# A 13x13 depthwise convolution on TensorE: from 18 matmuls a channel to 15, the two half-empty shifts joined into one

## What is computed

```python
def _L1_conv_ref(x, w_large, w_small, g_l, b_l, m_l, v_l, g_s, b_s, m_s, v_s, g_i, b_i, m_i, v_i):
    ...   # _dwconv: one filter per channel; _bn: scale and shift per channel
    kl = w_large.shape[-1]      # 13
    ks = w_small.shape[-1]      # 3
    out = _bn(_dwconv(x, w_large, kl // 2), g_l, b_l, m_l, v_l) + _bn(_dwconv(x, w_small, ks // 2), g_s, b_s, m_s, v_s) + _bn(x, g_i, b_i, m_i, v_i)
    return out

x = x + _L0_conv_ref(_gn(x), ...)
x = x + _L1_conv_ref(_gn(x), ...)
```

## Time and profile before

| | |
|---|---|
| median of 3 runs | 3048.57 us |
| the profiled execution's own time | 3045.88 us |
| its span, first to last instruction | 3044.2 us |
| busy share of the span: PE, DVE, ACT, POOL | 90%, 80%, 45%, 1% |
| mean granted TensorE clock | 0.981 of full speed |
| depthwise stage: PE's first matmul to the end | 2061.6 to 3044.2 us |
| mean DMA rate, 2170 to 2500 us | 280 GB/s |

### The profile page before, as it was taken

The page is one execution under the profiler, slowest core; times in us unless marked ns, Lnnn a source line. Parts: engine busy times, 40 slices in busy tenths (PEclk is TensorE's granted clock), DMA queues, the critical chain, the costliest instruction groups (busy, mean ns, idle before and its releaser), DMA issues. The chain is left out here.

```text
span 3044.2 us, 51281 instructions
## 1 busy us (share of the span) xinstructions
PE 2745.2 (90%) x18425; PEld 2007.7 (66%) x18425; DVE 2435.4 (80%) x3319; ACT 1382.1 (45%) x1729; POOL 29.0 (1%) x46
## 2 busy tenths in 40 slices
PE   0059999999999999999968999948999999999998
PEld 0036666666666666666645666637999999999997
DVE  7958999999999999999987898947565566666563
ACT  0044445555555555544224777745444444444442
POOL 0010000000000000000000000000000000000000
PEclk9999999999999999999989999969999999999999
DMA  9964111111111111110027999959988988999986
GB/s 336 416 212 150 49 64 62 65 66 62 66 67 60 66 68 59 66 61 16 16 75 236 340 344 345 348 169 281 288 281 281 282 272 279 278 286 279 286 248 186
DMA packets 228823, 564.24 MB, mean 185 GB/s; under 512 B 29248, under 2 KB 134464, under 8 KB 225600
## 3 DMA queue, kind: packets, MB, share of 16 engines
q1 hardware_dynamic: 211392, 495.41, 50.7%
q10 hardware_dynamic: 17280, 66.85, 5.8%
HBM read 402.21 MB, written 159.99 MB: 185 GB/s over the span
## 5 line engine op out<-in xcount | busy, mean ns | idle before, releaser
L1510 PE MATMUL cv_cb<-cv_hi,cv_toep 128*128 128x288 f16 (+1 forms) x4608 | 909.9, 290 | 31.6 <-DVE cv_lo L1444 28.8
L743 PE MATMUL qk_qb<-qk_xhi,whi 128*128 128x384 f16 x2592 | 846.9, 327 | 20.7 <-DVE qk_xlo L639 14.3
L743 PE MATMUL qk_qb<-qk_xlo,whi 128*128 128x384 f16 x2592 | 846.8, 327 | 0.0
L743 PE MATMUL qk_qb<-qk_xhi,wlo 128*128 128x384 f16 x2592 | 846.7, 327 | 0.0
L660 DVE SCALAR_TENSOR_TENSOR qk_dw<-qk_pool,qk_wd,qk_dw 128x768 f32<-128x768 f32 (+2 forms) x864 | 836.6, 1009 | 2.5 <-ACT qk_dw L528 2.4
L1510 PE MATMUL cv_cb<-cv_lo,cv_toep 128*128 128x288 f16 (+1 forms) x2304 | 667.6, 290 | 0.0
L1510 PEld LDWEIGHTS cv_cb<-cv_hi,cv_toep 128*128 128x128 f16 x4608 | 522.6, 113 | 91.7 <-DVE cv_lo L1444 28.9
L647 DVE TENSOR_REDUCE qk_pool<-qk_qb 128x192 f32<-128x768 f32 x432 | 412.0, 954 | 69.4 <-PE qk_qb L743 53.2
L1398 ACT ACTIVATE cv_res<-cv_cb,cv_cst 128x288 f32<-128x288 f32 x384 | 191.9, 501 | 555.3 <-PE cv_cb L1510 555.3
L1456 DVE COPY cv_rows<-cv_bb 128x512 f32<-128x512 f32 x216 | 145.7, 686 | 323.3 <-PE cv_bb L1491 323.3
L743 PEld LDWEIGHTS qk_qb<-qk_xhi,whi 128*128 128x128 f16 x2592 | 254.1, 98 | 184.3 <-DVE qk_xlo L639 17.8
(11 more groups left out here) (150 smaller groups left out, 2284.2 us busy)
## 6 DMA issues: line engine op xcount, KB each, us to landing
cv_toep<-toeplitz_scratch SPq DMA_DIRECT2D x384, 384.0 KB, 4.8
patch_scratch<-pr_turned SPq DMA_DIRECT2D x75, 832.0 KB, 9.5
cv_raw<-patch_scratch SPq DMA_DIRECT2D x24, 2600.0 KB, 10.7
st_x<-in_x SPq DMA_DIRECT2D x24, 2304.0 KB, 17.1
qk_xf<-in_x SPq DMA_DIRECT2D x72, 768.0 KB, 4.2
pr_xb<-in_x SPq DMA_DIRECT2D x24, 2304.0 KB, 10.0
out<-cv_rows ACTq DMA_DIRECT2D x72, 768.0 KB, 5.5
pr_vb<-v_scratch SPq DMA_DIRECT2D x24, 576.0 KB, 4.3
```

Source lines behind the costliest of these rows:

```text
L743: ins = nc.tensor.matmul(qbank[s % NQB][:, h, 0:2 * W], w[:, b, o * P:(o + 1) * P], x[:, par, j // 2, b, at_row:at_row + 2 * W], start=n = ...
L1510: ins = nc.tensor.matmul(out, toep[:, c % NTOEP, :].rearrange("p (s m v) -> p s v m", s=NS, m=P)[:, s, u * 2 + part], x[:, par, c, u:u + O ...
```

## The change

The depthwise stage runs 15 matmuls a channel. The padding of the Toeplitz layout is moved, and the partitions of a patch are ordered in two halves: the first 64 hold its first 4 rows, the last 64 the other 4. Shifts s = 0 and s = 1 stay as they are, 12 matmuls. What the third patch down still has to give are its first 4 rows, and they reach only the first 4 rows of the output. So for u = 0 and u = 1 these 64 partitions are put on top of each other, in `hi_last` and `lo_last`, and three matmuls with 128 input rows and 64 output columns (`late` taps) take the place of six.

- ACT copies `hi[0:64]` twice a quad into `hi_last`, DVE copies `lo[0:64]` twice a quad into `lo_last`; one of the two copies changes partitions.
- DVE writes the normalised channel into a new tile `norm` in the order channel, j, i; the border is zeroed by two instructions instead of four. `hi` and `lo` are made from `norm` and have one buffer each. The quad of a group is split when PE is done with the same quad of the group before (`free`), and quad 3 of group g in step g itself ("L3" second in ORDER).
- `toep` has 2048 bytes a partition instead of 3072; it is loaded in two halves of 64 partitions (1536 and 2048 bytes), `raw` too. `late` is one more load per quad, 128 partitions by 4 runs of 256 bytes.
- In the qkv stage POOL lays out the late taps, 6 copies for each of 16 offsets ix (the first 6 at the start), and SP sends them to DRAM, 6 transfers an offset in 256-byte runs, two offsets in each of units 2 to 9.
- POOL clears the part of `toep` that no load writes.

```diff
@@ stage_qkv, SyncE: at the end of a unit's step
+                if inner:
+                    for ix in (t * 2 - 4, t * 2 - 3):
+                        for b in range(CB):
+                            address(sp, ix * (HALF_ROWS * ERUN), 2)
+                            sp.wait_ge(late_made, ix * (2 * CB) + 2 * b + 2)
+                            for u in range(NU):
+                                windows = bass.AP(late, (b * NU + u) * EROWS * TW * 2,
+                                                  [[CB * NU * EROWS * TW * 2, P], [TW * 2, HALF_ROWS], [1, ERUN]])
+                                sp.dma_start(edge_dram[b * P:(b + 1) * P, u, bass.ds(ix, 1), :, :]
+                                             .rearrange("p a y n -> p (a y) n"), windows).then_inc(late_out[b], 16)
@@ stage_qkv, GpSimd
+            def late_taps(ix):
+
+                for b in range(CB):
+                    if not at(ix, 0):
+                        gp.wait_ge(late_out[b], ix * (16 * NU))
+                    for part in range(2):
+                        window = bass.AP(padw, (b * 2 + part) * KL * JX + (KL - ETAPS) * JX + ix,
+                                         [[CB * 2 * KL * JX, P], [TW, NU], [JX, ETAPS], [1, TW]])
+                        G.tensor_copy(late[:, b, :, 0:ETAPS, :, part], window).then_inc(late_made, 1)
@@ stage_depthwise, SyncE
+            def load_taps(g, c):
...
+                for h, skip in ((0, SKIP * RUN), (1, 0)):
+                    sp.dma_start(toep[h * HP:(h + 1) * HP, c % NTOEP, skip:KRUN],
+                                 bass.AP(v.tensor, v.offset, [[JR * RUN, TW], [RUN, HALF_ROWS], [1, KRUN - skip]])).then_inc(
+                                     toep_in[c % NTOEP], 16)
+
+            def load_late(g, q):
+
+                first = g * GRP + q * CPP
+                address(sp, first * (P * ERUN), 2)
+                sp.dma_start(late[:, q % NQUAD * CPP:(q % NQUAD + 1) * CPP, :],
+                             edge_dram[bass.ds(first, CPP)].rearrange("c u x y n -> (u x y) c n")).then_inc(
+                                 late_in[q % NQUAD], 16)
...
-                        sp.wait_ge(lo_done, g * NPC + NPC)
+                        sp.wait_ge(edge_done, g * NPC + NPC)
                         start.load_group(sp, g + 2, par)
                     if inner or g < NG:
...
+                        load_taps(g, c)
+                        if at(g, 0) and c < NQUAD:
+                            load_late(0, c)
+                        if c % CPP == CPP - 1 and not (at(g, 0) and c < NTOEP):
+                            load_late(g, c // CPP)
@@ ScalarE
-            SPLIT_AT = {2: 0, 5: 1, 8: 2, 11: 3}
+            SPLIT_AT = {3: 0, 7: 1, 11: 2}
+            LAST_AT = {4: 0, 8: 1, 12: 2}
...
+            def last_high(g, q):
+
+                act.wait_ge(hi_done, g * NPC + q + 1)
+                for u in range(NU):
+                    ins = nc.scalar.activation(hi_last[u * HP:(u + 1) * HP, part_of(q), :, 0:EI],
+                                               hi[0:HP, part_of(q), u:u + OJ, NS:TI], ACT.Copy)
+                ins.then_inc(hi_last_done, 1)
@@ VectorE
-                    V.tensor_scalar(raw[:, par, :, c, :], raw[:, par, :, c, :],
+                    V.tensor_scalar(piece[:, k].rearrange("p j i -> p i j"), raw[:, par, :, c, :],
                                     cst[:, bass.ds(g * GRP + c, 1), 0], cst[:, bass.ds(g * GRP + c, 1), 1],
                                     ALU.subtract, ALU.mult).then_inc(norm_done, 1)
...
+            def last_low(g, q):
+
+                dve.wait_ge(lo_done, g * NPC + q + 1)
+                for u in range(NU):
+                    ins = V.tensor_copy(lo_last[u * HP:(u + 1) * HP, part_of(q), :, 0:EI],
+                                        lo[0:HP, part_of(q), u:u + OJ, NS:TI])
+                ins.then_inc(lo_last_done, 1)
...
-            ORDER = ("N0", "B0", "B1", "N1", "B2", "L0", "B3", "N2", "B4", "B5", "L1", "N3", "B6", "B7", "B8", "L2", "L3")
+            ORDER = ("N0", "L3", "N1", "B0", "B1", "L0", "B2", "N2", "B3", "B4", "L1", "B5", "N3", "B6", "L2", "B7", "B8")
@@ TensorE: one channel
+                for u in range(NU):
+                    for k, (part, x) in enumerate(((0, hi), (0, lo), (1, hi))):
+                        nc.tensor.matmul(whole, taps[:, 0, u * 2 + part], x[:, c, u:u + OJ, 0:OI],
+                                         start=u == 0 and k == 0, stop=False, skip_group_check=True)
+                for part, x in ((0, hi_last), (0, lo_last), (1, hi_last)):
+                    nc.tensor.matmul(upper, few[:, part], x[:, c, :, 0:EI], start=False, stop=False, skip_group_check=True)
+                for u in range(NU):
+                    for k, (part, x) in enumerate(((0, hi), (0, lo), (1, hi))):
+                        ins = nc.tensor.matmul(whole, taps[:, 1, u * 2 + part], x[:, c, u:u + OJ, 1:1 + OI],
+                                               start=False, stop=u == NU - 1 and k == 2, skip_group_check=True)
+                ins.then_inc(conv_done, 1)
```

More of the change, by code:

```diff
@@ L621, in _ @@
             G.memset(blank[:, :], 0.0).then_inc(blank_made, 1)
+            G.memset(late[:, :, :, ETAPS:EROWS, :, :], 0.0).then_inc(late_zero, 1)
+            gp.wait_ge(pad_made, 1 + 2 * CB)
+            def late_taps(ix):
+                for b in range(CB):
+                    if not at(ix, 0):
[4 more added lines that the diff above has]
+                        G.tensor_copy(late[:, b, :, 0:ETAPS, :, part], window).then_inc(late_made, 1)
+            late_taps(0)
+            with gp.Fori(1, TW) as ix:
+                late_taps(ix)
         @block.vector
@@ L1253, in depthwise_start @@
     masked = ctx.enter_context(nc.semaphore("cv_masked"))
+    PITCH = NG * TI * GRP * TJ
     def load_group(sp, g, par):
[L1256 to L1257 removed]
+        for h in range(2):
+            v = patch_dram[h * HALF_ROWS:h * HALF_ROWS + 1, bass.ds(g, 1), :, :].rearrange("p a i n -> p (a i n)")
+            sp.dma_start(raw[h * HP:(h + 1) * HP, par].rearrange("p i c j -> p (i c j)"),
+                         bass.AP(v.tensor, v.offset, [[TH * PITCH, TW], [PITCH, HALF_ROWS], [1, TI * GRP * TJ]])).then_inc(raw_in[par], 16)
     def first_load(sp):
@@ L1295, in stage_depthwise @@
     NPIX = OI * OJ
+    EI = TI - NS
     with ExitStack() as ctx:
@@ L1369, in store, with split @@
                               rows[:, bd].rearrange("p y x -> p (y x)")).then_inc(out_done[bd], 16)
-            act.wait_ge(cst_in, 16)
-            SPLIT_AT = {2: 0, 5: 1, 8: 2, 11: 3}
-            def split(g, par, q):
-                act.wait_ge(edge_done, g * NPC + q + 1)
-                if not (isinstance(g, int) and g < 2):
-                    act.wait_ge(conv_done, g * GRP - 2 * GRP + (q + 1) * CPP)
-                nc.scalar.activation(hi[:, par, q * CPP:(q + 1) * CPP, :, 0:TI].rearrange("p c j i -> p (c j) i"),
-                                     raw[:, par, :, q * CPP:(q + 1) * CPP, :].rearrange("p i c j -> p (c j) i"),
-                                     ACT.Copy).then_inc(hi_done, 1)
-            for q in range(NPC):
-                split(0, 0, q)
+            def split(g, q):
+                act.wait_ge(edge_done, g * NPC + q + 1)
+                free(act, g, q)
+                nc.scalar.activation(hi[:, part_of(q), :, 0:TI].rearrange("p c j i -> p (c j) i"),
+                                     norm[:, q % 2].rearrange("p c j i -> p (c j) i"), ACT.Copy).then_inc(hi_done, 1)
+            def last_high(g, q):
[4 more added lines that the diff above has]
+                ins.then_inc(hi_last_done, 1)
+            for q in range(NPC - 1):
+                split(0, q)
+                last_high(0, q)
+            act.wait_ge(cst_in, 16)
             def step(g, par, inner=False):
@@ L1391, in step @@
                     return
+                split(g, NPC - 1)
                 if inner or g >= 2:
@@ L1475, in step @@
                         normalise(g + 1, 1 - par, n)
-                    elif kind == "L" and more:
-                        low(g + 1, 1 - par, n)
+                    elif kind == "L" and n == NPC - 1 and live:
+                        split(g, n)
+                    elif kind == "L" and n < NPC - 1 and more:
+                        split(g + 1, n)
             run(dve, step, tail=NG - 2)
@@ L1493, in back, with channel @@
                 ins.then_inc(back_done, 1)
+            def channel(g, c):
+                bank = cbank[c % NCB]
+                taps = toep[:, c % NTOEP, :].rearrange("p (s m v) -> p s v m", s=NS, m=P)
+                few = late[:, c % NTOEP, :].rearrange("p (m v) -> p v m", v=2)
+                whole = bank[:, 0:NPIX].rearrange("p (j i) -> p j i", j=OJ)
+                upper = bank[0:HP, 0:NPIX].rearrange("p (j i) -> p j i", j=OJ)[:, :, 0:EI]
+                for u in range(NU):
[9 more added lines that the diff above has]
+                ins.then_inc(conv_done, 1)
             def step(g, par, inner=False):
```

198 lines of the change are left out of this document (112 added, 86 removed).

## The result

| | median us | runs | lowest to highest |
|---|---|---|---|
| before | 3049.58 | 4 | 3047.66 to 3051.22 |
| changed | 3087.24 | 4 | 3076.01 to 3095.65 |

The ratio is 1.0121 (95%: 1.0086 to 1.0157): the change makes the kernel 1.2% slower, where 4.3% faster was forecast. The profiled execution took 3095.65 us, with a span of 3093.9.

The account below looks back on a forecast made before the run. PE was taken to bound the depthwise stage, the DMA engines next. From 3045.9 us, -142 (matmuls), +7 (group 0) and +4 (POOL) gave 2915, or 2917 us as median; range 2900 to 2978 us.

Parts of the forecast that it names:

- I price these like those that they replace: Depthwise stage on PE: the three joined matmuls cost 0.123 us each, so a channel falls from 2.28 to 1.91 us.
- -142 us: Depthwise stage on PE: 0.37 us saved a channel over 384 channels; a group goes from 40.34 to 34.4 us.
- a cost of switching between widths: Depthwise matmuls: possible objection to the price, dismissed because matmuls with 96 output columns among full ones show none.
- raw lands at T + 11.3 ... late taps at T + 15.1: Depthwise loads, steady groups: landing times counted from T, when PE ends channel 15; cost to the kernel 0.
- T + 17.9: Depthwise stage, steady groups: when PE wants the late taps for channel 8, T being PE's end of channel 15.
- rival 2: Depthwise loads: 256-byte packets bring late taps too late every group, PE stands 3 us a group; +68, 2985 us; chance 0.13.
- Group 0, +7: Depthwise stage, first group: PE waits 8.5 instead of 2.8 us before channel 8 and may lose clock; +7 us.
- POOL in the qkv stage, +4: qkv stage: POOL's late-tap copies hold up DVE, 0.5 us a unit; +4 us, bounds nothing and 29 us.
- DVE, 7.15 us a quad: Depthwise stage: DVE's work per quad, 34.1 us a group, just hidden by PE's 34.4.
- Rivals 1 and 4: Depthwise DVE: 1, slow copies make it the bound, 3034 us, chance 0.15; 4, all prices high, 3230 us, 0.04.
- rival 3: qkv stage: POOL holds DVE by its upper bound; +25, 2942 us; chance 0.05.
- ACT: Depthwise stage: ACT's work with eight added copies takes 20.5 of 34.4 us a group, hidden behind PE.

Follow-up runs that it names:

- e8: Changed kernel with the edits of e1 and e2 together, and the second half of raw sent ahead of channel 12's taps: 2904.27 us, ratio 0.9524.
- e11: Changed kernel with the edits of e1 and e5 together, places and order of the late loads untouched (wrong values): 2906.50 us, ratio 0.9533.
- e7: e2 with 96 output columns for 64 in the three joined matmuls, the 32 more being zero weights: 2976.35 us, ratio 0.9751.
- e5: Changed kernel with raw read in one transfer to 128 partitions, not two to 64 (wrong values): 2991.62 us, ratio 0.9808.
- e2: Changed kernel with sixteen places for eight in the late taps' tile and each late load sent one quad earlier: 3000.10 us, ratio 0.9845.
- e1: Changed kernel with 64 zero columns added to the three joined matmuls' weights, giving 128 output columns: 3109.92 us, ratio 1.0195.
- e4: Changed kernel with the three joined matmuls left out, their loads, copies and PE's waits for them kept: 3053.27 us, ratio 1.0017.

## Why the prediction was wrong

**Matmuls, "I price these like those that they replace".** Right for the stream (0.123 us apart among themselves), and 34.3 to 34.6 us a group, which the -142 us stand for, is what the kernel gets with equal widths (e8, e11). Wrong in "a cost of switching between widths ...": those rows have 96 columns, and 96 is not 64 (e7). The term left out is 0.24 us a channel, 92 us; with PE nearly without waits, 3000 to 2904 or 2906 is 94 to 96. The formula that the prediction sets against the rows (117.5 ns for 276 columns) is given by the Trainium skill, TensorE: Matmul & The Clock Gate, section "Back-to-back issue gap", for an isolated matmul, so the 123 ns of a stream do not contradict it.

**Loads, "raw lands at T + 11.3 ... late taps at T + 15.1", due "T + 17.9".** The packets of 256 bytes, about which I worried, weren't it: the late taps land 3.9 us behind `raw`, for 3.8 foreseen. `raw` was. I carried over its landing of 10.2 us from the earlier trace rows though the diff splits it in two transfers to 64 partitions; it took 15.3. (T + 0.8 + 10.2 is also T + 11.0 and not T + 11.3; the 0.3 had no row.) And SP came to it at T + 3.2 and not T + 0.8, with T at 2316.0 (2315.08 + 0.92): channel 7's taps, two transfers, began at 2316.98, and quad 1's late load stood ahead of `raw` too. So the taps landed at T + 22.4 (2326.41 + 11.95), and PE had come to channel 8 some 3 us before. The wait is rival 2's, with its size (2.9 us a group), but not with its cause, and what it brought beyond the wait, 25 us of clock, I had no term for in steady groups. e5 and e11 show that the rate of `raw` decides: at the old rate the order of the loads is good enough. The margin is thinner than the 2.8 us forecast: e11 still waits for late taps five times, up to 1.6 us, and SP comes late to `raw` there too (T + 3.8 in the group whose channel 15 ends at 2234.6).

**The sum.** Both terms together are 181 us, 3087 less e11's 2906. Their shares depend on the order in which they are taken away: late taps first (e2) 87 and then widths 94, `raw` first (e5) 96 and then widths 85, and the widths alone (e1) make it 23 slower. As those are differences of the same medians, that they add up is no check. Measured apart there are 92 us for widths, 62 of waiting, and clock: nine of the 21 returns begin with 1.60 to 1.63 us for six matmuls, and such a return costs some 2.7 us (6.20 us from 2423.14 on, 3.51 for the same work from 2297.34 on), an estimated 24. 2906 + 92 + 62 + 24 = 3084. The waits and returns are those of the profiled execution, which took 3095.65, so some 10 us of it have no term.

**Group 0, +7.** Channel 8 was to begin at 2087.5 and began at 2088.50, but that is in part luck. PE began the stage at 2057.50, not at 2061.6, and stood twice: 4.6 us before channel 2, for taps, which no term foresaw, and 4.8 us before channel 8, for the late taps, where 8.5 were forecast. From PE's start to channel 8 it is 31.0 us for 25.9 forecast and 23.2 before. The chain:
```profile
2052.44 15.38 DMA cv_toep<-toeplitz_scratch
2067.86 1.63 PE cv_cb L1610 x6
...
2076.38 11.91 DMA cv_late<-toeplitz_edge_scratch
...
2088.50 1.60 PE cv_cb L1610 x6
```

**POOL in the qkv stage, +4.** No cost shows: PE has 497.55 of 500 us against 497.67, and the stage's last reduction begins at 1558.6 us for 1561.4. No experiment took POOL's copies away. This, and not group 0, is why e11 is at 2906 and not at 2917: its depthwise stage starts at 2055.26 us where it was 2061.59, 6.3 us earlier and not 4 later, and from there to the end of the span (2904.9) it takes 133.0 us less, for the 135 forecast (142 - 7). What makes the stages ahead of it shorter no run shows.

**DVE, 7.15 us a quad.** Measured 5.55. Normalising (0.615), border and low part were sized right within 0.1 us; the copies take 456 ns for my 1.26 us. The rule of the Trainium skill, VectorE: DVE Perf Modes, section "Mode 4×_2P", that I set aside for the nearest row gave an estimated 0.4, and the trace's 0.456 agrees with it. Rivals 1 and 4, which need a slow DVE, fell with it; rival 3 fell with the qkv stage above. **ACT** was right (1.12 us a copy for 1.06).

## What to carry to other kernels

Read what a diff does to the shape of every transfer and operand, not only to its bytes: here a transfer to half of the partitions ran at 217 GB/s for 362 to 371, and matmuls with 64 output columns among ones with 128 cost 0.24 us for going there and back, which zero columns avoided at no price that the times show (e8, e11). A row prices only its own shape; 96 columns said nothing of 64. Before counting a saving on the engine that bounds, look for a load whose sending hangs on that engine's progress and whose landing it needs within the same turn: in such a loop the saving became a wait, and the wait cost clock on top (e1, e4).

## What the hardware showed that I had not expected

- Width 64 among 128: 0.09 us ahead of the first narrow matmul, 0.03 behind, and the same on the way back; width 96: nothing.
- Transfers to 64 partitions: 217 GB/s, to 128: 362 to 371.
- PE's clock after a wait: in e1_wide all of the steady waits (about 7 us) ended at 1.2 GHz, 1.63 us for six matmuls; in the changed kernel, with waits of about 3 us, nine of 21 ended so, ten at 2.4 GHz (1.63 and 0.93), and two lie between. Its runs differ by 20 us, those of e8_both_spread by 2.
